# A routing front end moved into the attention before it: batch 0's scores, picks, count and lists made between attention units

## The chip, the cores and the metric

The kernel runs on one NeuronCore of a Trainium2 chip. The metric is the device time in microseconds (us) of one execution. Engines are named as the profile names them: PE is the matrix engine (TensorE; PEld is its load of stationary weights), DVE the vector engine, ACT the scalar engine, POOL the GpSimd engine and SP the engine that issues most DMAs. They run side by side, each its own list of instructions in order, and meet through semaphores.

## The reference

Two batches of 1024 tokens with 256 features go through four layers, each added to its input:

```
x = x + attention0(layernorm(x), ctx)      # 16 heads, 77 context tokens
x = x + slot_mixture(layernorm(x))         # 16 experts, 1024 slots
x = x + attention1(layernorm(x), ctx)      # "second attention": 16 heads, 77 keys
x = x + top3_mixture(layernorm(x))

top3_mixture(x):
  a = x @ P_w.T                            # 64 address features
  dw1, dw2, dw3 = route(a @ U1.T), route(a @ U2.T), route(a @ U3.T)   # 12 experts
  h = gelu(sum_e dw1[:, e] * (x @ W1[e].T))     # 256 -> 1024
  y = sum_e dw2[:, e] * (h @ W2[e].T)           # 1024 -> 256
  return y + dw3 @ b2
route(z): softmax over the 3 largest of 12, zero elsewhere
```

## The kernel before, in words

The tokens are 16 tiles of 128 (8 for each batch), held in `X` for the whole program. The four layers are stages that follow each other. This change is about the end of the third and the beginning of the fourth.

**Second attention** (`attention("a1_", ...)`). A unit is one token tile. There are 16 units; in unit u the tile is u // 2 of batch u % 2, so the batches alternate. Units 4 to 13 stand in a hardware loop, the others are written out. The work of three units overlaps. In step u each engine does, in this order:

- PE (`step`): `scores` of unit u (L827, into `psS`), `input_T` of unit u + 1 (L810), two parts of `probs_T` of unit u - 1 (L843), `output_T` of unit u - 2 (L862), `values` and the last part of `probs_T` of unit u - 1 (L852, L843), `queries` of unit u + 1 (L817), `project` of unit u - 2 (L872).
- DVE (`step`): the four maxima over the scores and their subtraction for unit u (L600, L606), `normalise` of unit u - 1 (L619, L621), `norm_in` of unit u + 2 (L584), `residual` and `stat` of unit u - 2 (L628, L632).
- ACT: copies out of PSUM, the exponential of unit u (L732), then the biased queries of unit u + 1 (L725), which the scores of unit u + 1 need.
- POOL adds the output bias to each tile of `X` (L705) once its normalised input is made.

After unit 15's `probs_T` comes a tail with no next unit to overlap. There DVE also makes the normalisation factors of 14 tiles (`next_begin`, L676), ahead of `normalise` of unit 15. SP loads the weights `W1` of the mixture's first product during this stage.

**The front end of the top-3 mixture** (`route_vector`, `route_tensor`, `route_scalar`, `route_gpsimd`, `route_sync`). A new block of instructions begins when all engines have ended the attention. DVE normalises 16 tiles into `xn` (L1931); PE transposes them (L2005) and multiplies them with the router product `PU` (L2014), two tiles at a time; SP stores `xn` to memory, 1 MB for each batch. For batch 0 DVE then picks the three largest of 12 scores (`pick`, L1604 to L1612), sums the choices (`choose`), PE counts them with triangular and all-ones matrices (`count`, L1622, L1626), DVE works out each token's place in lists sorted by expert (`lists`, L1635 to L1674), compares places with counters (`match_two`, L1713), and PE multiplies these comparisons (`add_tokens`, L1720) so that the list of tokens appears in `psF`. `found_tokens` (L1727 to L1729) turns it into indices and releases POOL, which gathers the rows of `xn` from memory (L1909). Where PE would have nothing to do it runs filler products on weights that nobody reads (`turn_over`, L89).

**The first product** (`expand`, L2133) begins when the first two gathered blocks have been transposed (L2111). It goes through 54 blocks of 128 rows, 8 matmul passes each. What batch 1 needs (picks, count, lists) is made on DVE while batch 0's blocks are multiplied.

## Time and profile before

| | |
|---|---|
| three runs | 1085.78, 1088.67 (median), 1090.91 us |
| profiled execution | 1091.19 us, of which span 1089.3 |
| PE busy | 1038.6 us (95%) |
| DVE busy | 642.7 us (59%) |
| ACT, POOL busy | 401.3 (37%), 282.8 (26%) |
| mean granted PE clock | 0.983 of full |

The span is the time from the first to the last instruction in the trace; the program's own time is 1.9 us longer. A time with a decimal point such as 566.59 is a moment counted from the span's start. The second attention runs from about 447 to 566.6, the front end from 566.6 to 600.3. The granted clock has two levels, 2.4 GHz (1.00 in the rows) and 1.2 GHz (0.50); a value between them is a stretch that held both.

### The profile page before, as it was taken

How to read it: one execution, taken by the hardware profiler on the slowest of the kernel's cores; microseconds unless marked ns; L12 is line 12 of the kernel's file. 1: busy time of each engine (PE TensorE's matmuls, PEld its weight loads, DVE VectorE, ACT ScalarE, POOL GpSimd, SP SyncE). 2: the span in 40 equal slices, each digit the busy share in tenths (PEclk: the TensorE clock that was granted, in tenths of full speed). 3: DMA queues.
4: the chain of work that ended last, by engine and by line, in shares of the span. 5: the costliest groups of instructions: out<-in, count | busy, mean ns of one | idle time of the engine just before them, and what ended most of it. 6: DMA issues, size and time to landing. Idle time of an engine off the chain costs nothing. (4 is left out here: it accounts for less than half of the span.)

```text
span 1089.3 us, 20108 instructions
## 1 busy us (share of the span) xinstructions
PE 1038.6 (95%) x6560; PEld 751.5 (69%) x6560; DVE 642.7 (59%) x1450; ACT 401.3 (37%) x784; POOL 282.8 (26%) x306
## 2 busy tenths in 40 slices
PE   7999989999899999999998999998999999899996
PEld 3788854588899888688875444443347777577784
DVE  3998857777444544567768888665421366534512
ACT  0566644432111222266642355554343222122230
POOL 1211110000021100211111322255533677454431
PEclk8999999999899999999999999999999999999998
DMA  7000040000399200470002444489999999674634
GB/s 232 2 1 0 1 174 18 0 2 1 124 348 343 79 1 0 192 280 0 0 7 90 153 168 174 172 285 358 341 352 405 407 329 346 215 254 146 218 122 169
DMA packets 72057, 177.17 MB, mean 163 GB/s; under 512 B 10605, under 2 KB 31071, under 8 KB 70444
## 3 DMA queue, kind: packets, MB, share of 16 engines
q1 hardware_dynamic: 47362, 102.09, 25.5%
q0 software_dynamic: 20896, 69.75, 18.9%
q10 hardware_dynamic: 3722, 4.33, 1.2%
q8 instruction: 46, 0.75, 0.3%
q14 instruction: 31, 0.25, 0.1%
HBM read 126.06 MB, written 47.97 MB: 160 GB/s over the span
## 5 line engine op out<-in xcount | busy, mean ns | idle before, releaser
L2133 PE MATMUL f_psH<-W,ctxT 128*128 (+2 forms) x216 | 100.6, 610 | 3.9 <-DVE f_stage L2328 2.0
L2232 ACT ACTIVATE shared<-f_psH 128x512 f32<-128x512 f32 x108 | 62.8, 597 | 108.0 <-PE f_psH L2133 75.7
L2182 PE MATMUL f_psT<-W,f_xg 128*128 (+1 forms) x432 | 99.2, 383 | 1.9 <-DVE shared L2477 1.8
L2182 PE MATMUL f_psT<-W,sel 128*64 (+2 forms) x432 | 98.6, 381 | 2.3 <-ACT sel L2257 1.4
L2133 PE MATMUL f_psH<-W,f_xTk 128*128 (+2 forms) x216 | 97.8, 595 | 1.7 <-DVE f_stage L2328 1.0
L2477 DVE COPY shared<-f_psT 128x256 f32<-128x256 f32 x54 | 22.7, 421 | 123.2 <-PE f_psT L2182 97.8
L1909 POOL DMA_INDIRECT f_xg<-xn_d,f_toks x54 | 56.3, 1042 | 130.2 <-PE f_psT L2111 102.4
L2182 PEld LDWEIGHTS f_psT<-W,f_xg 128*128 128x128 f32 (+1 forms) x432 | 79.8, 190 | 13.5 <-issue 3.5
L2182 PEld LDWEIGHTS f_psT<-W,sel 128*64 128x64 f32 (+2 forms) x432 | 62.9, 150 | 27.5 <-issue 5.7
L1909 POOL DMA_INDIRECT f_temps<-h_d,f_toks x54 | 52.8, 979 | 94.6 <-PE f_psH L2161 70.2
L1515 POOL DMA_DIRECT2D m_eos<-m_eo x32 | 16.8, 525 | 201.9 <-DVE m_eo L1412 200.6
L2133 PEld LDWEIGHTS f_psH<-W,ctxT 128*128 128x128 f32 (+2 forms) x216 | 33.9, 167 | 50.5 <-issue 50.5
L2133 PEld LDWEIGHTS f_psH<-W,f_xTk 128*128 128x128 f32 (+2 forms) x216 | 35.8, 175 | 44.7 <-issue 44.6
L705 POOL TENSOR_TENSOR X<-X,a_bob 128x256 f32 x32 | 24.4, 765 | 162.7 <-DVE a_xn L584 82.8
L2068 POOL DMA_INDIRECT p_d<-shared,f_dest x54 | 55.7, 1031 | 34.9 <-DVE shared L2477 20.0
L2257 ACT ACTIVATE sel<-f_psH 128x512 f32<-128x512 f32 x54 | 29.3, 594 | 93.7 <-PE f_psH L2161 93.7
L2257 ACT ACTIVATE f_xg<-f_psH 128x512 f32<-128x512 f32 x54 | 29.3, 595 | 89.8 <-PE f_psH L2161 89.8
L2182 PE MATMUL f_psT<-f_stage,sel 128*32 128x256 f32 (+1 forms) x464 | 62.3, 381 | 0.0
L2410 DVE SCALAR_TENSOR_TENSOR a_W<-f_g,f_wt,a_W 128x1024 f32<-128x1024 f32 x32 | 41.1, 1285 | 34.8 <-DMA f_g<-p_d,f_rows 34.3
L1909 POOL DMA_INDIRECT f_g<-p_d,f_rows x48 | 55.8, 1163 | 20.2 <-issue 13.4
L2161 PE MATMUL f_psH<-ident,f_temps 128*128 128x128 f32 x432 | 57.5, 276 | 2.8 <-DMA f_temps<-h_d,f_toks 1.9
L2161 PEld LDWEIGHTS f_psH<-ident,f_temps 128*128 128x128 f32 x432 | 48.5, 141 | 16.1 <-issue 10.6
(339 smaller groups left out, 2246.6 us busy)
## 6 DMA issues: line engine op xcount, KB each, us to landing
p_d<-shared SPq DMA_DIRECT2D x54, 512.0 KB, 3.3
W<-in_f_W1T SPq DMA_DIRECT2D x12, 1024.0 KB, 17.2
W<-in_f_W2T SPq DMA_DIRECT2D x12, 1024.0 KB, 11.0
m_wg<-in_m_Wg SPq DMA_DIRECT2D x16, 512.0 KB, 4.3
m_wu<-in_m_Wu SPq DMA_DIRECT2D x16, 512.0 KB, 5.7
m_wd<-in_m_Wd SPq DMA_DIRECT2D x16, 512.0 KB, 6.2
h_d<-a_W SPq DMA_DIRECT2D x16, 512.0 KB, 5.9
f_g<-p_d SPq DMA_DIRECT2D x8, 384.0 KB, 7.8
```

The costliest lines, as they stand in the source:

```text
L705: pool.tensor_tensor(X[:, s, j], X[:, s, j], bob[:, :], ALU.add).then_inc(xb_ready, 1)
L1515: pool.dma_start(eos[s * SL:(s + 1) * SL, b, j, :], eo[b * SL:(b + 1) * SL, s, :]).then_inc(eo_moved[s], 16)
L1909: pool.indirect_dma_start(place, None, source, bass.IndirectOffsetOnAxis(ap=index, axis=0)).then_inc(done, 16)
L2068: pool.indirect_dma_start(p2_rows[b], bass.IndirectOffsetOnAxis(ap=dest[:, b * TB + i:b * TB + i + 1], axis=0), y_out[:, n % OUTS, :], Non ...
L2133: mm = pe.matmul(psH[at, n % 2, c, :], xTk[n % 2][:, k, at], weights, start=k == 0, stop=k == KD - 1)
L2161: mm = pe.transpose(psH[:, n % 2, h, k * P:(k + 1) * P], hg[:, n % SEATS, (h * KQ + k) * P:(h * KQ + k + 1) * P], ident[:, :])
L2182: mm = pe.matmul(psT[at, n % 2, 0:D], hT[n % 2][:, k, at], weights, start=k == 0, stop=k == KH - 1)
L2232: act.activation(po[:, n % 2, c * HH:(c + 1) * HH], psH[:, n % 2, c, :], ACT.Copy).then_inc(po_ready, 1)
L2257: act.activation(hT[n % 2][:, h * KQ:(h + 1) * KQ, :].rearrange("p k n -> p (k n)"), psH[:, n % 2, h, :], ACT.Gelu).then_inc(hT_ready, 1)
L2410: sums.step(dve.scalar_tensor_tensor(h, rows_k, wt[:, 0, k, u:u + 1], h, ALU.mult, ALU.add))
L2477: dve.tensor_copy(y_out[:, n % OUTS, :], psT[:, n % 2, 0:D]).then_inc(yo_ready, 1)
```

## The change

The second attention now takes its units batch by batch: unit u is tile u % 8 of batch u // 8, all 16 units written out. An object `Early` is called at fixed places of the unit steps and does batch 0's part of the front end there:

- the router weights are centred (DVE, step 1) and multiplied to `PU` (PE, step 2), so that scores can be made from the raw `X` and scaled afterwards by each token's inverse deviation;
- in steps 3 to 10 PE transposes the finished tile u - 3 of batch 0 along with `output_T`, ACT copies 512 columns where it copied 256, and in steps 4 to 11 PE multiplies a tile with `PU` into free columns of `psO`;
- DVE, after `stat` of the step: factors of batch 0 (step 9), scaling and the first pick (11), second pick (12), third pick and `choose` (13), the starts of the lists (14), shifts and places (15); the count is made by PE in step 14, which waits for `choose`;
- four small constant loads go ahead of `W1` in SP's queue.

In the front end's own block DVE normalises only tiles 0 to 4 and the last two, POOL the other nine; DVE goes at once to `match_two`; PE transposes and scores only batch 1, between its `add_tokens`. All but two fillers go. The first product's second block waits for the copy of batch 1's scores.

The PE's order in an attention step, before (a step of the loop) and then now (the fifth step, unit 4); `a_psP`, `a_psO` and the like are the attention's PSUM and SBUF tiles, and `f_PU` is the router product:

```order
L827 MATMUL a_psS<-shared,a_qT 128x154 x8
L810 MATMUL a_psA<-ident,a_xn 128x128 x2
L843 MATMUL a_psP<-ident,a_pr 128x128 x6
L862 MATMUL a_psP<-ident,a_o 128x128 x2
L852 MATMUL a_psO<-shared,a_pT 128x51 x2
L843 MATMUL a_psP<-ident,a_pr 128x128 x3
L843 MATMUL a_psP<-ident,a_pr 80x128
L852 MATMUL a_psO<-shared,a_pT 128x51 x8
L817 MATMUL a_psA<-a_xnT,a_W 128x128 x4
L872 MATMUL a_psP<-a_W,a_oT 128x256 x2
```
```order
L869 MATMUL a_psS<-shared,a_qT 128x154 x8
L852 MATMUL a_psA<-ident,a_xn 128x128 x2
L885 MATMUL a_psP<-ident,a_pr 128x128 x6
L906 MATMUL a_psP<-ident,a_o 128x128 x2
L911 MATMUL a_psP<-ident,X 128x128 x2
L1913 MATMUL a_psO<-f_PU,a_oT 128x36 x2
L896 MATMUL a_psO<-shared,a_pT 128x51 x2
L885 MATMUL a_psP<-ident,a_pr 128x128 x3
L885 MATMUL a_psP<-ident,a_pr 80x128
L896 MATMUL a_psO<-shared,a_pT 128x51 x8
L859 MATMUL a_psA<-a_xnT,a_W 128x128 x4
L921 MATMUL a_psP<-a_W,a_oT 128x256 x2
```

Two transposes of `X` and two products with `f_PU` have come between `output_T` (L862, now L906) and the first `values` (L852, now L896).

DVE's order at the end of the attention: before from the last step's `residual` on, and now from the last rows of `lists` on (`f_pdiv` and `f_pmod` are what `match_two` compares):

```order
L628 TENSOR_TENSOR X<-a_psP,X 128x256
L632 BN_STATS stats<-X 128x6
L297 MEMSET mhalf 128x2x7
L298 TENSOR_TENSOR mean<-stats 128x2x7
L299 TENSOR_TENSOR mdif<-stats 128x2x7
L300 TENSOR_TENSOR veps<-stats 128x2x7
L302 TENSOR_SCALAR mean<-mean 128x2x7
L303 SCALAR_TENSOR_TENSOR mdif<-mdif 128x2x7
L305 SCALAR_TENSOR_TENSOR vars<-veps,mdif 128x2x7
L308 TENSOR_SCALAR veps<-vars 128x2x7
L619 RECIPROCAL a_rsum<-a_psO 128x16
L621 TENSOR_TENSOR a_o<-a_psO,a_rsum 128x256
```
```order
L1738 CAST f_pdiv<-f_part 128x24
L1739 CAST f_pmod<-f_part 128x24
L301 MEMSET mhalf 128x6
L302 TENSOR_TENSOR mean<-stats 128x6
L303 TENSOR_TENSOR mdif<-stats 128x6
L304 TENSOR_TENSOR veps<-stats 128x6
L306 TENSOR_SCALAR mean<-mean 128x6
L307 SCALAR_TENSOR_TENSOR mdif<-mdif 128x6
L309 SCALAR_TENSOR_TENSOR vars<-veps,mdif 128x6
L312 TENSOR_SCALAR veps<-vars 128x6
L638 RECIPROCAL a_rsum<-a_psO 128x16
L642 TENSOR_TENSOR a_o<-a_psO,a_rsum 128x256
```

Ahead of the block of norm factors (L297 to L308, now L301 to L312) stand now the 23 instructions of `shifts` and `places`, of which the last ones are shown; `normalise` of unit 15 (L619, now L638) stands behind both.

PE's order in the front end, from the end of the count up to the first transposes of gathered rows (L2111, now L2257):

```order
L89 MATMUL f_psT<-W 128x512 x8
L1720 MATMUL f_psF<-f_temps 128x28 x6
L89 MATMUL f_psT<-W 128x512
L1720 MATMUL f_psF<-f_temps 128x28 x6
L89 MATMUL f_psT<-W 128x512
L1720 MATMUL f_psF<-f_temps 128x28 x12
L89 MATMUL f_psT<-W 128x512 x3
L2111 MATMUL f_psT<-ident,f_xg 128x128 x4
```
```order
L89 MATMUL f_psN<-a_W 128x512 x2
L1785 MATMUL f_psF<-f_temps 128x28 x6
L2164 MATMUL f_psT<-ident,f_stage 128x128 x4
L1785 MATMUL f_psF<-f_temps 128x28 x6
L2164 MATMUL f_psT<-ident,f_stage 128x128 x4
L2173 MATMUL f_psH<-f_PU,f_stage 128x36 x4
L1785 MATMUL f_psF<-f_temps 128x28 x6
L2164 MATMUL f_psT<-ident,f_stage 128x128 x4
L2173 MATMUL f_psH<-f_PU,f_stage 128x36 x4
L1785 MATMUL f_psF<-f_temps 128x28 x6
L2164 MATMUL f_psT<-ident,f_stage 128x128 x4
L2173 MATMUL f_psH<-f_PU,f_stage 128x36 x8
L2257 MATMUL f_psT<-ident,f_xg 128x128 x4
```

The fillers on `W` are gone, and batch 1's transposes (L2164) and scores (L2173) stand between the `add_tokens` (L1720, now L1785) of batch 0.

The diff, cut to its core:

```diff
+                def at(j, s):
+
+                    return (s, j) if first else divmod(B * j + s, NT)
...
+                                early.evict(dve, u, room)
...
+                                early.vector(dve, u, stat_done)
...
+                            add_biases(0, NT + 4)
+                            early.power(pool)
+                            add_biases(NT + 4, TT)
...
+                            if routed(u - 1):
+                                pe.wait_ge(y_done, u)
+                                for k in range(KD):
+                                    mm = pe.transpose(psP[:, 0, (KD + k) * P:(KD + k + 1) * P],
+                                                      X[:, 0, u - 1, k * P:(k + 1) * P], ident[:, :])
...
+                    PLACES = 6
+                    CENTRE, PRODUCT, FACTORS, PICKS, COUNT = 1, 1, 9, 11, 13
...
+                    def tensor(self, pe, u, room, oT, oT_ready):
+                        if u == self.PRODUCT:
+                            pe.wait_ge(pw_step, 3)
+                            for k in range(KD):
+                                mm = pe.matmul(room[:, k * R * E1:(k + 1) * R * E1], Pw[:, k * P:(k + 1) * P], U[:, :],
+                                               start=True, stop=True)
+                            mm.then_inc(pu_mm, 1)
+                        i = u - 3
+                        if 0 <= i < NT:
+                            pe.wait_ge(oT_ready, u - 1)
+                            pe.wait_ge(pu_ready, 1)
+                            for k in range(KD):
+                                mm = pe.matmul(room[:, self.column(i)], oT[:, u % B, KD + k, :], PU[:, k, :],
+                                               start=k == 0, stop=k == KD - 1)
+                            mm.then_inc(z0_mm, 1)
+                        if u == self.COUNT:
+                            pe.wait_ge(consts, 2)
+                            count(pe, room, chosen_ready, 1).then_inc(count_mm, 1)
...
+                    def evict(self, dve, u, room):
+                        if u == self.PRODUCT:
+                            dve.wait_ge(pu_mm, 1)
+                            dve.tensor_copy(PU[:, :, :].rearrange("p k n -> p (k n)"), room[:, 0:KD * R * E1]
+                                            ).then_inc(pu_ready, 1)
+                        if u == self.PLACES + 2:
+                            self.copy_scores(dve, room, 0, self.PLACES)
+                        if u == NT + 2:
+                            self.copy_scores(dve, room, self.PLACES, NT)
+                        if u == self.COUNT:
+                            dve.wait_ge(count_mm, 1)
+                            steps_of.step(dve.tensor_copy(counts[:, :], room[:, 0:(NT + 1) * E1]), hold=False)
...
+                        if u == self.CENTRE + 2:
+                            dve.wait_ge(ld, 16 * 4)
+                            one.step(dve.tensor_tensor(
+                                under[:, :, :], iota[:, 0:E1 + 1].unsqueeze(2).to_broadcast([P, E1 + 1, E1]),
+                                iota[:, 0:E1].unsqueeze(1).to_broadcast([P, E1 + 1, E1]), ALU.is_gt))
+                        if u == self.FACTORS:
+                            dve.wait_ge(stat_done, NT)
+                            begin0(dve)
+                        if u == self.PICKS:
+                            end0(dve)
+                            dve.wait_ge(z0_ready, 2)
+                            one.step(dve.tensor_tensor(
+                                Z[:, :, 0:NT, :], Z[:, :, 0:NT, :],
+                                rstd[:, 0:NT].unsqueeze(1).unsqueeze(3).to_broadcast([P, R, NT, E1]), ALU.mult))
+                        if self.PICKS <= u < self.PICKS + TOP:
+                            pick(dve, one, 0, 0, 0, NT, range(u - self.PICKS, u - self.PICKS + 1))
+                        if u == self.PICKS + TOP - 1:
+                            choose(dve, one, 0, 0)
+                            dve.sem_inc(chosen_ready, 1)
+                        if u == self.COUNT + 1:
+                            one.hold()
+                            starts(dve, one, counts)
+                        if u == self.COUNT + 2:
+                            shifts(dve, one, counts)
+                            places(dve, one, 0, 0)
+
+                second_attention(Early())
...
+                    BY_VECTOR = 5
+                    SHARES = ((BY_VECTOR, NT - BY_VECTOR), (BY_VECTOR + 2, TT - 2 - BY_VECTOR))
...
                     def route_vector(dve, one):
 
-                        def norm_in(u):
-                            dve.tensor_scalar(xn[:, u, :], Xf[:, u, :], mean[:, u:u + 1], rstd[:, u:u + 1],
-                                              ALU.subtract, ALU.mult).then_inc(xn_ready, 1)
-
-                        for u in range(2):
-                            norm_in(u)
+                        for u in range(BY_VECTOR):
+                            norm_in(dve, u, xn_ready)
                         begin(dve)
-                        for u in range(2, NT - 1):
-                            norm_in(u)
-                        end(dve)
-                        for u in range(NT - 1, TT):
-                            norm_in(u)
-                        dve.wait_ge(ld, 16 * 4)
-                        one.step(dve.tensor_tensor(
-                            under[:, :, :], iota[:, 0:E1 + 1].unsqueeze(2).to_broadcast([P, E1 + 1, E1]),
-                            iota[:, 0:E1].unsqueeze(1).to_broadcast([P, E1 + 1, E1]), ALU.is_gt))
-                        dve.wait_ge(z_mm, NT // 2)
-                        one.step(dve.tensor_copy(Z[:, :, 0:NT, :].rearrange("p r t e -> p t r e"),
-                                                 psZ[:, 0, 0:HZ].rearrange("p (t r e) -> p t r e", r=R, e=E1)))
-                        pick(dve, one, 0, 0, 0, NT)
-                        choose(dve, one, 0, 0)
-                        dve.sem_inc(chosen_ready, 1)
-                        dve.wait_ge(count_mm, 1)
-                        lists(dve, one, psN, 0, 0)
                         for i in range(0, NT, 2):
                             match_two(dve, i, at_hit, iota, pdiv, at_used).then_inc(hit_ready, 2)
                             match_two(dve, i, at_row, iota, pmod, at_used).then_inc(row_ready, 2)
...
                         for i in range(NT):
                             act.wait_ge(hit_ready, i + 1)
                             wait(act, at_used, i - AR + 1)
                             act.activation(at_tile[:, i % AR, :, 0, :], at_hit[:, i % AR], ACT.Copy, scale=tokid[:, i:i + 1]
                                            ).then_inc(tile_ready, 1)
+                            if i % 2:
+                                inputs_T(i // 2)
+                        act.wait_ge(z_mm, NT // 2)
+                        act.activation(Z[:, :, NT:TT, :].rearrange("p r t e -> p t r e"),
+                                       psZ[:, 0, 0:HZ].rearrange("p (t r e) -> p t r e", r=R, e=E1), ACT.Copy
+                                       ).then_inc(z_copied, 1)
...
+                        for u in range(BY_VECTOR, NT):
+                            norm_in(pool, u, xn_by_pool)
                         power(pool)
-                        pool.memset(ones_b[:, :], 1.0).then_inc(consts, 1)
-                        pool.wait_ge(ld, 16 * 4)
-                        pool.tensor_copy(below_b[:, :], below).then_inc(consts, 1)
+                        for u in range(NT, TT - 2):
+                            norm_in(pool, u, xn_by_pool)
...
+                        turn_over(pe, psN[:, :], W_flat, 2)
                         pe.wait_ge(w1_ld, 16 * E1)
-                        pe.wait_ge(consts, 2)
-                        count(pe, psN, chosen_ready, 1).then_inc(count_mm, 1)
-                        turn_over(pe, psT[:, 0, :], W, 8)
                         for i in range(NT):
                             pe.wait_ge(row_ready, i + 1)
                             pe.wait_ge(tile_ready, i + 1)
                             add_tokens(pe, i, 1, psF, at_used)
-                            if i % 2 and i < NT - 3:
-                                turn_over(pe, psT[:, 0, :], W, 1)
+                            if i % 2:
+                                inputs_T(i // 2)
+                                if i > 1:
+                                    scores(i // 2 - 1)
+                        scores(NT // 2 - 1)
 
```

## Rows read from the trace of the kernel before

**Rows 1.** Windows: stretch, length, busy PE PEld DVE ACT POOL, PE clock, DMA share, GB/s
```profile
483.49:551.53 68.04, 66.92 (x621) 58.75 (x620) 48.42 (x99) 41.10 (x90) 6.86 (x10) 1.00 0.00 0
551.53:566.59 15.06, 13.64 (x100) 10.76 (x99) 8.70 (x25) 5.48 (x12) 2.60 (x1) 1.00 0.00 1
566.59:600.30 33.71, 28.66 (x167) 18.38 (x168) 28.02 (x104) 8.53 (x20) 6.05 (x8) 0.93 0.26 81
```
**Rows 2.** Timeline, one loop unit: start, length, engine, line, operation, idle before
```profile
483.73 0.42 DVE L628 TENSOR_TENSOR X<-a_psP,X 128x256 f32 x1 [0.81 <-PE a_psP L872]
...
484.65 1.62 DVE L600 TENSOR_REDUCE a_mx<-a_psS 128x4 f32<-128x308 f32 x4
...
485.69 0.55 PE L852 MATMUL a_psO<-shared,a_pT 128*128 128x51 f32 x4
...
486.30 1.44 DVE L606 TENSOR_TENSOR a_sc<-a_psS,a_mx 128x1232 f32<-128x1232 f32 x1
...
487.94 1.23 ACT L732 ACTIVATE a_pr<-a_sc 128x1232 f32<-128x1232 f32 x1 [0.56 <-DVEq L612]
...
488.56 0.26 DVE L619 RECIPROCAL a_rsum<-a_psO 128x16 f32<-128x16 f32 x1 [0.81 <-PE a_psO L852]
...
489.20 0.41 DVE L584 TENSOR_SCALAR a_xn<-X,mean,rstd 128x256 f32 x1
...
489.60 0.63 ACT L725 ACTIVATE a_qT<-a_psA,a_bq 128x128 f32<-128x128 f32 x2 [0.43 <-PE a_psA L817]
...
490.28 0.81 PE L827 MATMUL a_psS<-shared,a_qT 32*128 32x154 f32 x16
```
**Rows 3.** Timeline, a unit outside the loop
```profile
476.68 0.81 PE L827 MATMUL a_psS<-shared,a_qT 32*128 32x154 f32 x16
...
477.58 1.62 DVE L600 TENSOR_REDUCE a_mx<-a_psS 128x4 f32<-128x308 f32 x4
```
**Rows 4.** Timeline: first gather, first two blocks of the first product
```profile
594.96 1.16 POOL L1909 DMA_INDIRECT f_xg<-xn_d,f_toks  x1 [23.27 <-DVEq L1959]
...
600.30 4.88 PE L2133 MATMUL f_psH<-W,ctxT 128*128 x8 [0.29 <-issue]
...
605.24 3.60 PE L2133 MATMUL f_psH<-W,f_xTk 128*128 x8
```
**Rows 5.** Timeline, weight loads of two successive score groups, front end
```profile
571.45 0.97 PEld L2014 LDWEIGHTS f_psH<-f_temps,f_stage 128*128 128x128 f32 x8
...
572.73 0.97 PEld L2014 LDWEIGHTS f_psH<-f_temps,f_stage 128*128 128x128 f32 x8
```
**Rows 6.** Timeline, DVE: factors, picks, choices, list starts, shifts
```profile
567.26 0.15 DVE L298 TENSOR_TENSOR mean<-stats 128x2 f32<-128x2 f32 x1
...
575.71 0.25 DVE L1604 TENSOR_REDUCE f_wt<-f_temps 128x8 f32<-128x96 f32 x1
...
581.87 0.17 DVE L1635 TENSOR_SCALAR f_cnt<-f_psN 128x12 f32<-128x12 f32 x1 [0.67 <-PE f_psN L1626]
...
584.21 0.15 DVE L1645 TENSOR_SCALAR f_base<-f_start 128x1 f32<-128x1 f32 x1
...
587.18 0.46 DVE L1667 TENSOR_TENSOR f_temps<-f_temps,sel 128x288 f32<-128x288 f32 x1
```
**Rows 7.** Timeline, DVE: unit 15 is normalised, attention's tail
```profile
561.74 0.26 DVE L619 RECIPROCAL a_rsum<-a_psO 128x16 f32<-128x16 f32 x1 [2.42 <-PE a_psO L852]
```
**Rows 8.** Timeline, DVE: two successive pairs of comparisons
```profile
589.04 0.33 DVE L1713 TENSOR_TENSOR f_temps<-f_iota,f_pdiv 128x168 f16<-128x168 f32 x1
...
590.16 0.33 DVE L1713 TENSOR_TENSOR f_temps<-f_iota,f_pdiv 128x168 f16<-128x168 f32 x1
```
**Rows 9.** Timeline, POOL: a bias added, two factors raised to a power
```profile
476.18 0.73 POOL L705 TENSOR_TENSOR X<-X,a_bob 128x256 f32 x1 [6.12 <-DVE a_xn L584]
...
568.30 0.92 POOL L315 TENSOR_TENSOR rstd<-veps,mhalf 128x2 f32<-128x2 f32 x1 [6.30 <-DVE veps L308]
```
**Rows 10.** Timeline, ACT: two comparisons are scaled
```profile
589.47 0.62 ACT L1985 ACTIVATE f_temps<-f_temps,f_tokid 128x84 f16<-128x84 f16 x2 [9.12 <-DVE f_temps L1713]
```

207 lines of the change are left out of this document (137 added, 70 removed).

## The prediction

> **What bounds the kernel now.** I read the windows first, to see which engine fills each stretch, and then single units of the timeline, to see what releases what. In the ten loop units of the second attention (483.49 to 551.53) [rows 1] PE is busy 66.92 of 68.04 us, DVE 48.42. A unit costs 6.8 us, and at first sight DVE has 2 us free in each. The unit itself says otherwise [rows 2]: the reader is to follow one chain through three engines. The reduction starts at 484.65, the exponential 3.29 us later, it lasts 1.23, ACT's two query copies can start then, and the next scores follow 0.68 behind their start (489.60 to 490.28). So the next scores come at the earliest 3.29 + 1.23 + 0.68 = 5.2 us behind the reduction. The copies started 0.43 us behind the exponential's end, released by PE: the chain is that close to binding. Outside the loop [rows 3] the reduction starts 0.90 us behind its own scores, so chain (6.1) against PE (6.8) leaves 0.7 us. The written-out form is what the new kernel has.
>
> The front end, from 566.59 [rows 1], lasts 33.71 us and is a line on DVE: 28.02 us busy. Its end is the first gather at 594.96, 28.4 us in, and the first block of the product 5.3 us later [rows 4].
>
> **PE in the attention.** Eight times two transposes and two products with `PU` are added. Two score groups of two tiles, with the transposes between them, stand 1.28 us apart (571.45 to 572.73) [rows 5], so a tile costs 0.64 us: 8 x 0.64 = 5.1 us. They stand in PE's own list, which has no room to hide them. The product `PU` itself I take as 0.3 us (bounds 0 and 0.5: four passes like those of rows 5). The copies that ACT makes longer stay beside PE's work. The four constant loads go ahead of `W1` on SP, and nothing before the front end waits for `W1`: nothing.
>
> **DVE in the attention.** All pieces stand between `stat` and the next reduction. Free are 0.7 us of them; what goes beyond delays the next scores one for one. A second delay in a row is smaller, since PE ends `project` while it waits and the next `residual` is then early.
>
> - Step 9, factors: 567.26 to POOL's release at 568.30, 1.04 us [rows 6, 9]. PE's unit is 0.64 longer there, so it hides.
> - Step 11: scaling 0.46 (row 587.18, the same 288 elements) and a pick. Three picks and `choose` are 19 instructions from 575.71 to 581.20 (581.87 less the 0.67 of waiting for PE), 0.29 each [rows 6]. A pick of six is 1.74. Together about 2.25 us: the reduction is 3.15 behind its scores, the unit lasts 3.15 + 5.2 = 8.35: +1.55.
> - Step 12: six more, 1.74. DVE has ended `norm_in` 4.2 us behind its reduction (3.09 to the subtraction's end, 1.05 for `normalise` and `norm_in`) [rows 2], at 7.35; with 0.92 for `residual` and `stat` and the 1.74 the reduction stands at 10.0 - 8.35 = 1.65: the unit is 6.85: nothing.
> - Step 13: seven instructions, 2.0 us. The reduction of step 14 is 2.9 us late in its unit. PE comes to the count 2.2 us in, as it comes to `values` now (485.69, scores 0.24 ahead of 483.73 [rows 1, 2]), waits 0.8 and counts; DVE waited 0.67 for a count with both signals [rows 6], of which I take 0.5 (bounds 0 and 0.67): the unit is 8.15: +1.35.
> - Step 14: list starts, 581.87 to 584.21, 2.34 us [rows 6]. The last reduction is 3.3 us behind its scores in place of 0.9.
> - Step 15: shifts and places, 584.21 to 589.04, 4.83 us [rows 6, 8], and then the 1.04 of factors, all ahead of `normalise` of unit 15. Counted from the last scores: subtraction's end 6.4, `normalise` 7.1, `residual` and `stat` 8.05, shifts and places 12.9, factors 13.95. Now this `normalise` starts at 561.74 [rows 7], 10.2 behind the scores at 551.53. Here ends last not PE but DVE: +3.7.
>
> DVE's sum is 1.55 + 1.35 + 3.7, rounded 6.7 with the copies that `evict` adds, and the attention grows by 5.1 + 0.3 + 6.7 = 12.1 us.
>
> **The front end.** Counted from its start, five normalisations are 1.7 us (two now take 566.59 to 567.26 [rows 1, 6]), factors to 2.7. Pairs of comparisons follow 1.12 apart [rows 8], the last done at 7.2. But PE's list is in order and mixes batch 1 in. `inputs_T` of its first tiles waits for POOL's fifth normalisation. The trace has no such operation on POOL; its two-input add of the same shape takes 0.73 [rows 9], the nearest row, which I take. Bounds: DVE's 0.41 for the same work [rows 2], and twice 0.73. Three by 2.3, the power of 0.92 us behind the factors at 3.7, the fifth at 5.2. Then transposes to 5.8 (0.3 to 0.5 us, the 1.28 of rows 5 less the products), ACT's copy to 6.5 (taken as long as two scalings, 0.62 [rows 10]), its two scalings to 7.1, two `add_tokens`, the second transposes and first scores to 8.8, ACT's next two scalings to 9.2, again adds, transposes, scores to 10.9, last scalings 11.3, last adds 11.6; the indices and the gather at 12.75. Before it was 28.4: -15.6 us. With POOL at 0.41 it is 0.6 us better, at 1.46 3.9 worse (the ninth normalisation then comes at 14.1). The store of `xn` can start by 2.5 and has ten microseconds. Gather to product stays 5.3: batch 1's last scores end at about 13.9, before the gathered rows land.
>
> On POOL the Trainium skill, "GPSIMD Engine Reference", "Engine selection", says that two-input elementwise work runs at about half VectorE's speed and one-input work at roughly line rate. The trace agrees on the first (0.73 against DVE's 0.42 for an add) and no run here shows the second; by that rule the lower bound would hold, and the sum be 0.6 us better.
>
> **The sum.** +12.1 - 15.6 = -3.5 us. Behind the first block nothing changes: PE fills what follows, and the DVE work for batch 1 hangs on the same list. Against the profiled execution, 1091.19 us (span 1089.3 and 1.9 around it), that is 1087.7; the median of the three runs is 2.5 us lower, so the forecast is 1085.2 us. A measurement of this kernel can't tell less than 0.5%, 5.4 us, from no change.
>
> **The rivals.**
>
> *The DVE pieces hide.* For it: 20 us idle in the ten units. If PE absorbs steps 11 to 14 (the reduction may be late where PE has other work), the attention pays PE's 5.4, the count's 0.5, and in the tail shifts, places and factors from 6.5 to 12.4 against 10.2, 2.2 us: 8.1. Then 8.1 - 15.6 = -7.5, 1081.2 us: faster. Against it: the 0.43 us of rows 2.
>
> *The clock falls.* The front end has a mean granted clock of 0.93 [rows 1], so part of it ran at 1.2 GHz, and the first block behind it, after a stretch with little PE work, took 4.88 us where the next took 3.60 [rows 4]. The fillers that stood there are gone, and the attention's end gets new holes of 2.4 and 3.7 us. If the clock is low from the attention's tail to the second block: about 6 us of PE's serial work in the tail at half speed, half of it on the path, +3; fillers, adds, two transposes and two score groups on the way to the list, 4.4 us, doubled, +4.4; one more slow block, 3.6 in place of the 1.28 lost now, +2.3. From -3.5 to +6.2: 1094.9, slower. It decides from a fall before the front end; a fall only behind the list costs at most the 2.3. Against it: the tail now has 1.4 us of PE idle [rows 1] at clock 1.00.
>
> The Trainium skill, "TensorE: Matmul & The Clock Gate", "HAM oscillation — how this bites in real kernels", has gaps in TensorE's work throttle it again, and each return is paid anew. The trace agrees that the clock falls in the stretch with the thin work [rows 1, 4]; by the rule this rival's price is due.
>
> *The list was not what the front end waited for.* If the store of `xn`, or POOL's other work, or a slow POOL holds the gather, most of the gain is lost: with POOL at 1.46 us the sum is +0.4, 1089.1. For it: nine normalisations are moved to an engine that reads the same memory as DVE; against: DVE's own list was 28 us long and its end released the gather.
>
> **How the numbers follow.** Forecast 0.55, its own range 1081.5 to 1089.5; hidden pieces 0.22; clock 0.12; POOL or store 0.11. Faster by over 0.5%: the hidden case and 0.07 of the forecast's edge, 0.29. Slower: the clock case and 0.01, 0.13. Within: 0.58. The range reaches to the hidden case's far side and the clock case: 1078.5 to 1094.
>
> **What would show it.** The attention, from the scores of unit 4 to the block change, 12 us longer, with units of 7.4 us in steps 4 to 10, two of over 8 us in steps 12 and 14, and `normalise` of unit 15 behind DVE's factors instead of released by PE. The first gather 12 to 13 us into the front end, PE's adds waiting for ACT's scalings, POOL's normalisations 0.7 us each. Wrong would be: units that stay at 6.8; a last `normalise` released by PE; a clock of 0.50 before the front end.

## The result, and the profile after

The changed kernel is slower: 1097.75 us (median of five runs, 1090.70 to 1100.31) against 1088.67; the ratio is 1.0062, 95% interval [1.0032, 1.0091]. The forecast was 1085.2 with a range to 1094.0. Repeated twice with twelve runs each, the same kernel gave 1.0039 [1.0016, 1.0061] and 1.0047 [1.0027, 1.0067]. So it is slower by 0.4 to 0.6%, where a gain of 0.3% was forecast. One execution of the first kernel with fillers (1200.87 us, mean granted clock 0.841) and one of the first kernel with split normalisations (1114.59 us, 0.969) are left out of the ratios below.

The kernel before was run again beside each kernel, and its median moved from 1088.67 up to 1105.10 us between these sets, so ratios are compared below, and times only within one set.

The profiled execution took 1090.70 us, span 1088.5, which is less than before's 1089.3. The other four runs took 1096.2 to 1100.3, with mean granted clocks of 0.970 to 0.973 where the profiled one had 0.981. This profile shows one part of the loss; the other needs a profile of a longer execution, which came with the repetition.

First the attention. These rows are PE's of the changed kernel: scores of units 10, 11, 13, 14 and 15, and the first instruction of the front end.

```profile
521.13 0.81 PE L869 MATMUL a_psS<-shared,a_qT 32*128 32x154 f32 x16
528.64 0.81 PE L869 MATMUL a_psS<-shared,a_qT 32*128 32x154 f32 x16
...
544.17 0.81 PE L869 MATMUL a_psS<-shared,a_qT 32*128 32x154 f32 x16 [1.31 <-ACT a_qT L763]
551.07 0.81 PE L869 MATMUL a_psS<-shared,a_qT 32*128 32x154 f32 x16
559.23 0.81 PE L869 MATMUL a_psS<-shared,a_qT 32*128 32x154 f32 x16
...
577.66 1.95 PE L89 MATMUL f_psN<-a_W 128*128 128x512 f32 x4 [0.30 <-PEq L569]
```

A middle unit lasts 7.51 us (528.64 less 521.13; 6.8 before [rows 1]), step 12 lasts 8.22 (544.17 less 535.95; forecast 8.35), step 13 lasts 6.90 (551.07 less 544.17; forecast 6.85), step 14 lasts 8.16 (forecast 8.15), and the tail from the last scores to the front end 18.43 (15.06 before). From the first scores (449.21; 450.80 before) to the front end it is 128.45 us against 115.79: +12.7, where the sum had +12.1.

Then the windows of the changed kernel (columns: stretch, length, then busy time and, in brackets, number of instructions of PE, PEld, DVE, ACT and POOL, granted clock, DMA share, GB/s) and PE's timeline in the front end.

```profile
577.66:583.50 5.84, 2.30 (x10) 0.93 (x10) 5.71 (x19) 0.62 (x2) 5.81 (x5) 1.00 0.18 60
583.50:600.73 17.23, 12.39 (x70) 11.08 (x71) 8.11 (x26) 4.95 (x13) 12.39 (x12) 0.51 0.40 129
600.73:604.50 3.77, 3.77 (x5) 1.70 (x6) 3.32 (x14) 0.13 (x1) 1.85 (x2) 0.51 0.36 107
```

```profile
582.05 0.35 PE L1785 MATMUL f_psF<-f_temps 128*128 128x28 f16 x6 [2.44 <-DVE f_temps L1778]
586.36 1.11 PE L2164 MATMUL f_psT<-ident,f_stage 128*128 128x128 f32 x4 [3.96 <-POOL f_stage L2102]
588.50 0.49 PE L1785 MATMUL f_psF<-f_temps 128*128 128x28 f16 x6 [1.03 <-ACT f_temps L2134]
588.84 1.10 PE L2164 MATMUL f_psT<-ident,f_stage 128*128 128x128 f32 x4
589.72 1.76 PE L2173 MATMUL f_psH<-f_PU,f_stage 128*128 128x36 f32 x8
...
600.73 5.52 PE L2281 MATMUL f_psH<-W,ctxT 128*128 x8 [0.30 <-issue]
```

PE stood 3.96 us before its first transposes, released by POOL's normalisation, and from 583.5 on it ran at 1.2 GHz (0.51): the scores of two tiles took 1.76 us in place of 0.98 (the row below is of before), the first block 5.52 in place of 4.88 [rows 4].

```profile
571.55 0.98 PE L2014 MATMUL f_psH<-f_temps,f_stage 128*128 128x36 f32 x8
```

The first gather started 17.8 us into the front end and the first block 23.1, in place of 12.75 and 18.1. So the front end gave 10.6 us (33.71 less 23.07), not 15.6.

POOL's normalisations answer to the 0.73 of [rows 9]. One line for all nine (durations in ns, minimum, median, maximum), and the two slowest from the timeline:

```profile
L2102 POOL TENSOR_SCALAR f_stage<-X,mean,rstd x9: 1213/1222/2566, 577.7 to 589.9; 128x256 f32<-128x256 f32 x9
```

```profile
582.54 2.57 POOL L2102 TENSOR_SCALAR f_stage<-X,mean,rstd 128x256 f32<-128x256 f32 x1
...
589.90 1.66 POOL L2102 TENSOR_SCALAR f_stage<-X,mean,rstd 128x256 f32<-128x256 f32 x1
```

The one of 2.57 us ran while DVE made comparisons (from 580.76 to 584.2), the one of 1.66 beside DVE's last pair. Those for which DVE stood still took 1.21 to 1.22.

Between the two profiled executions +12.7 (attention), -10.6 (front end) and +0.6 (first block) make +2.6 us. The rest of the 0.8 by which the changed span is the shorter one lies in code that is the same in both: 1.6 ahead of the first scores, 1.9 behind the second block.

### The profile page after: what moved, and what is told of

The parts are those of the page before. It is cut to its first block and busy times, and to the rows that moved or that the text cites. A ratio compares the mean times of both kernels' runs of the same rounds, so it can differ in the third digit from the quotient of the medians.

```text
span 1088.5 us, 19787 instructions
## 1 busy us (share of the span) xinstructions
PE 1030.2 (95%) x6534; PEld 750.4 (69%) x6534; DVE 641.4 (59%) x1456; ACT 399.1 (37%) x779; POOL 295.7 (27%) x316
## 5 line engine op out<-in xcount | busy, mean ns | idle before, releaser
L2625 DVE COPY shared<-f_psT 128x256 f32<-128x256 f32 x54 | 22.7, 422 | 124.6 <-PE f_psT L2330 99.2
L2215 POOL DMA_INDIRECT p_d<-shared,f_dest x54 | 55.6, 1030 | 34.2 <-DVE shared L2625 19.4
L2085 POOL DMA_INDIRECT f_g<-p_d,f_rows x48 | 54.6, 1137 | 17.6 <-issue 12.8
L1414 PE MATMUL m_psE<-m_eos,m_wu 128*128 128x256 f32 x256 | 57.8, 380 | 0.4 <-DVE m_wu L1490 0.4
```

What stands on the lines that cost most here:

```text
L1414: mm = pe.matmul(psY[:, s, 0:D], ecT[:, s, c, :], eos[:, s, c, :], start=c == 0, stop=c == CS - 1)
L2085: pool.indirect_dma_start(place, None, source, bass.IndirectOffsetOnAxis(ap=index, axis=0)).then_inc(done, 16)
L2215: pool.indirect_dma_start(p2_rows[b], bass.IndirectOffsetOnAxis(ap=dest[:, b * TB + i:b * TB + i + 1], axis=0), y_out[:, n % OUTS, :], Non ...
L2625: dve.tensor_copy(y_out[:, n % OUTS, :], psT[:, n % 2, 0:D]).then_inc(yo_ready, 1)
```

## The experiments

Two theories. **A, the clock:** the attention's tail and the front end hold too little work for PE, the granted clock falls to half, and the longer executions have more of it. **B, POOL:** its slow normalisations hold PE and the list. Each ratio is to the kernel before, with its 95% interval, of twelve runs where nothing else is said. Times "in" count from the start of the front end.

**The changed kernel again, twice.** No edit.

> The changed kernel once more, unaltered. Its four runs without a profile were at 1096.2 to 1100.3 us with a mean granted clock of 0.970 to 0.973, the profiled one at 1090.7 us with 0.981. Theory A (the clock: the front end falls to half clock, and most runs hold a further stretch of it that the profiled one did not have): the median stays at 1096 to 1100 us, mean clocks again fall into two groups, and a profile from the slow group shows a stretch of 15 to 25 us at 0.50 that the first profile does not have. Theory B (GpSimd's slow normalisations alone cost the time): one group of clocks and the same median. Here the two are only told apart if the profile comes from the slow group.

> The changed kernel unaltered, for its groups of runs beside those of the next two on one chip. Theory A: two groups again, 6 us apart, the slower with mean clocks 0.005 lower; if the profile falls into it, it shows the half clock for 13 us from PE's 1.92 us wait on, and 22.5 us from the last scores to the front end in place of 18.4. Rival: a slow profile with a short fall in the tail, and the missing clock elsewhere.

The first gave nine runs from 1091.5 to 1094.2 (mean clocks 0.975 to 0.978) and three from 1098.3 to 1098.9 (0.972 to 0.974); its profile came from the faster ones and looks like the first (18.44 us from the last scores to the front end). The second gave six runs of 1090.5 to 1095.6 and six of 1096.6 to 1099.1 (0.970 to 0.974), and its profile, 1097.07 us, fell among the latter. In the mean the groups are 6.1 and 4.2 us apart (expected: 6). Its windows around the tail, and PE in it:

```profile
559.00:568.90 9.90, 7.77 (x67) 6.46 (x67) 8.16 (x23) 4.93 (x9) 0.00 (x0) 1.00 0.01 2
568.90:582.40 13.50, 12.93 (x45) 9.98 (x46) 7.70 (x38) 2.40 (x6) 1.33 (x1) 0.52 0.00 0
```

```profile
561.11 0.81 PE L869 MATMUL a_psS<-shared,a_qT 32*128 32x154 f32 x16
...
568.77 0.95 PE L885 MATMUL a_psP<-ident,a_pr 128*128 128x128 f32 x6 [1.92 <-ACT a_pr L770]
...
571.83 3.49 PE L896 MATMUL a_psO<-shared,a_pT 128*128 128x51 f32 x16
575.12 2.04 PE L921 MATMUL a_psP<-a_W,a_oT 128*128 128x256 f32 x4
...
579.95 3.45 PE L89 MATMUL a_psS<-a_W 128*128 128x512 f32 x4
583.69 1.96 PE L89 MATMUL f_psN<-a_W 128*128 128x512 f32 x4 [0.30 <-PEq L569]
```

PE waits 1.92 us for the last exponents, and then its clock is 1.2 GHz for 13 us: products that take 2.00 us at full speed take 3.49, and the front end starts 22.58 us behind the last scores in place of 18.43: 4.15 us. In the first profile the same wait was followed by the same fall, but for 3 us only:

```profile
567.50:570.50 3.00, 3.00 (x18) 2.89 (x16) 2.72 (x15) 1.27 (x4) 0.00 (x0) 0.53 0.00 0
570.50:577.66 7.16, 5.97 (x30) 3.89 (x29) 4.32 (x21) 1.02 (x3) 1.33 (x1) 1.00 0.00 0
```

There it cost nothing, since DVE's shifts and places ended last anyway: with the clock at 1.00 throughout the tail is as long, 18.43 us (below). Of the ten profiles taken with this wait left open, five had the short fall and five the long one. The long fall explains the mean clocks too: 10.5 us more at half clock are 0.005 of the span. What makes it long or short in one execution I did not find. The front ends of the two profiles are alike (first gather 17.8 us in both). Their spans differ by 6.4 us: 4.15 in the tail, 1.9 ahead of the first scores (451.07 against 449.21), in code that no kernel here changes and where the profiles range from 448.6 to 451.9, and the small rest behind the tail.

**POOL's normalisations on DVE.**

```
-  BY_VECTOR = 5
+  BY_VECTOR = NT              # all of batch 0 on DVE
   for i in range(0, NT, 2):   # ahead of each pair of comparisons
+      if i < NT - 2:
+          for u in range(NT + i, NT + i + 2):
+              norm_in(dve, u, xn_ready)
-  for u in range(BY_VECTOR, NT):
-      norm_in(pool, u, xn_by_pool)
-  for u in range(NT, TT - 2):
-      norm_in(pool, u, xn_by_pool)
```

> All 16 normalisations of the front end on VectorE (8 of the first batch, then 2 of the second batch ahead of each pair of comparisons), none on GpSimd. Theory B: PE's first transposes no longer wait for GpSimd (3.96 us in the changed kernel's profile), the list is ready when VectorE's chain allows (8 x 0.42 + 1.1 + 3 x 2.0 + 1.2 = 11.7 us, so first gather about 14 us into the front end in place of 17.8), and the median falls by 3 to 4 us. Theory A: the clock stays at 0.50 from about 6 us into the front end, the pairs on PE still take 3.2 us each, the gather comes 16 to 17 us in, and the median falls by 1 us or less.

1.0000 [0.9978, 1.0022], median 1089.61 where the changed kernel beside it had 1092.76. PE's wait for POOL is gone and the gather is at 14.05 us in (591.51 less 577.46):

```profile
583.07 0.64 PE L2160 MATMUL f_psT<-ident,f_stage 128*128 128x128 f32 x4
584.74 0.49 PE L1785 MATMUL f_psF<-f_temps 128*128 128x28 f16 x6 [1.03 <-ACT f_temps L2137]
585.07 1.09 PE L2160 MATMUL f_psT<-ident,f_stage 128*128 128x128 f32 x4
...
591.51 1.16 POOL L2085 DMA_INDIRECT f_xg<-xn_d,f_toks  x1 [9.37 <-DVEq L2121]
```

The transposes show the clock fall between 583 and 585. B's 3 to 4 us are there (3.7 in the gather, 3.15 in the medians), and with them the change costs nothing; A alone would have given 1 or less.

**Fillers in the front end.** Passes over weights that nobody reads, with POOL's normalisations kept, and then with them on DVE.

```
-  turn_over(pe, psN, W_flat, 2)
+  turn_over(pe, psN, W_flat, 4)      # with DVE's normalisations: 7
   ...
+  turn_over(pe, psN, W_flat, 4)      # behind the second addition (POOL's form only)
   scores(NT // 2 - 1)
+  turn_over(pe, psN, W_flat, 1)
```

> Idle stretches of PE in the front end filled with multiplications of weights that nobody reads: 2 more passes (1 us each) before the first addition of tokens, 4 after the second, 1 at the end; GpSimd keeps its normalisations. Theory A: the granted clock stays at 1.00 through the front end, a pair on PE takes 1.9 us in place of 3.2, the first gather comes 3 to 4 us earlier (14 to 15 us in), the first block takes 4.9 us in place of 5.5, and the median falls by 4 to 8 us, the runs' mean clocks rising above 0.98. Theory B: the gather still waits for GpSimd's last normalisation (it ends 13.8 us in), so it comes at 15 us at the earliest, the clock alone saves 1 to 2 us.

> Both edits: all normalisations on VectorE, and 5 more filling passes on PE before the first addition (PE would wait about 5 us there), 1 at the end. If both theories hold their parts add: the gather comes 13 to 14 us in, the first block starts 20 us into the front end (23.1 in the changed kernel) and takes 4.9 us, and the median falls by 4 to 6 us, to 1092 to 1094. If only the clock counts, it equals the kernel with fillers alone; if only GpSimd counts, the kernel with VectorE's normalisations alone.

1.0051 [1.0023, 1.0080] and 1.0002 [0.9972, 1.0032]: no gain over the same kernels without fillers, where A had 4 to 8 us. But neither kernel is the test that it was meant to be, since the clock did not stay up until the gather. It stood at 1.00 for the first 9 us or more and then fell. With POOL's normalisations (first two rows) it fell about where PE waited 1.24 us for POOL, and with DVE's (last two) between 590 and 592; the scores of two tiles, 0.98 us at full clock, then took 1.76:

```profile
596.12 1.12 PE L2164 MATMUL f_psT<-ident,f_stage 128*128 128x128 f32 x4 [1.24 <-POOL f_stage L2102]
597.02 1.76 PE L2173 MATMUL f_psH<-f_PU,f_stage 128*128 128x36 f32 x8
```

```profile
592.17 1.08 PE L2160 MATMUL f_psT<-ident,f_stage 128*128 128x128 f32 x4
593.05 1.76 PE L2169 MATMUL f_psH<-f_PU,f_stage 128*128 128x36 f32 x8
```

The gather came at 18.35 us in with POOL's normalisations and at 14.07 with DVE's (17.8 and 14.05 without fillers). So a full clock ahead of the third pair of tiles is worth nothing, as PE then waits for POOL between the pairs (0.24, 1.24) or for DVE. What the half clock costs behind it comes from a later kernel: from the third transposes to the gather it is 3.82 us in the changed kernel (591.61 to 595.43) and 3.13 in the last form below, at full clock. With POOL on the path the clock is thus worth about 0.7 us there, an estimate from these two profiles; no run kept POOL's normalisations and held the clock. The filler behind the last scores stood in the way of the gathered tokens: gather to first block took 6.05 us in both, in place of 5.3 and 5.4. Both profiles also had the 13 us fall in the tail (22.7 and 22.6 us).

**The tail.** First PE's 1.92 us wait filled, alone and with DVE's normalisations; then also the wait for the last normalised output, which was then 1.68 us long.

```
+  turn_over(pe, psA, Wq, 2)
   probs_T(NT - 1, B - 1, U - 1, 0)
   ...
+  turn_over(pe, psA, Wq, 2)          # second form only
   output_T(NT - 1, B - 1, U - 1, 4 * U)
```

> One edit to the changed kernel: PE's wait of 1.92 us for the last unit's exponents, in the attention's tail, is filled with two passes over weights that nobody reads. Theory A (that wait drops the clock: for 3 to 4 us in two profiles, for 13 us in the profiles of the two kernels with fillers in the front end, whose attention is the same): the clock stays at 1.00 to the end of the attention, the front end starts 0.5 to 1.5 us earlier than in the profiles with the short fall (577.0 in place of 577.7 to 579.0), the slower group of runs (3 of 12 at 1098.3 to 1098.9, the rest 1091.5 to 1094.2) thins out, and the median falls by 1 to 2 us. Rival (the half clock follows from the idle time in the units ahead, or from the clock's own rhythm): it falls all the same, no change in start or median.

> All normalisations on VectorE and the tail's wait filled. The two effects add if both are real: VectorE's normalisations alone gave 1089.6 (median) against 1092.8 of the changed kernel; with the tail's clock held it should be 1087.5 to 1088.5, and its upper group of runs (1092.7 to 1094.7, 3 of 12) gone. If the filler does nothing: 1089.6 again.

> The changed kernel with both of PE's waits in the attention's tail filled, two passes each over weights that nobody reads: the one for the last exponents (1.92 us) and the one for the last normalised output (1.68 us once the first is filled, and where the clock then fell for 4 us). Theory A: the clock stays at 1.00 up to the front end, the time from the last scores to the front end is 18.4 to 18.7 us (18.4 with the short fall of the changed kernel's profile, 19.8 with the first wait filled alone, 22.7 where the fall was 13 us long), the runs lose their slower group (upper end below 1096, mean clocks above 0.976), and the median is 1 to 4 us below the changed kernel's in proportion to before (ratio about 1.003 or less). Rival (the slow group is made elsewhere): the same two groups as before, ratio 1.004 to 1.006.

One wait filled: 1.0058 [1.0027, 1.0088] (seven runs) and 1.0020 [0.9999, 1.0041], no gain in either, against the forecasts of 1 to 2 us each. The clock stayed up through the filled wait and fell in the next one, where a fall is on the path: 19.80 and 19.79 us from the last scores to the front end. Both filled: 18.43 us, at full clock throughout:

```profile
560.00:577.94 17.94, 16.67 (x102) 11.64 (x95) 14.20 (x55) 5.53 (x12) 1.33 (x1) 1.00 0.00 1
```

and 1.0030 [1.0005, 1.0055]. Thirteen of the changed kernel's 29 runs had a mean clock below 0.975; with both waits filled, three of twelve. The intervals overlap, so the gain in time is not shown by this ratio alone. And the low clocks are not all gone, as was expected: two of the twelve were at 1115 us and 0.971, so the tail is not the only place where time at half clock comes and goes.

**Shifts and places to the front end,** in the changed kernel and with the first wait filled.

```
-  if u == self.COUNT + 2: shifts(...); places(...)   # attention, step 15
   begin(dve)
+  shifts(dve, one, counts)                           # front end
+  places(dve, one, 0, 0)
```

> One edit to the changed kernel: the first batch's shifts and places (22 VectorE instructions, 4.9 us) leave the attention's last step and stand in the front end, ahead of the comparisons. If they cost the attention what the sum said (3.7 us in the tail), the front end starts at 573.5 to 574.5; there the first comparison comes 4.9 us later on VectorE, but PE waits for GpSimd's normalisations until 8.7 us in and to 13.8 us in anyway, so the gather moves little (18 to 20 us in) and the median falls by 1.5 to 3.5 us. If they were hidden in the attention (rival), the start stays at 577.7 and the median rises by 1 to 5 us. If the clock follows PE's wait in the tail, the low stretch there goes too, since the last exponents no longer... stand behind that work: no effect either way, as the work is issued after them.

> The changed kernel with shifts and places in the front end and PE's 1.92 us wait filled. From the last scores to the front end: 15.06 us before, 18.43 in the changed kernel. If shifts and places carry the whole difference, as the prediction's sum had it, 14.8 to 15.1 us. If the starts in the step ahead carry part (they put the last reduction off, and with it the exponents, for which PE waits until 7.67 us after the scores in place of 5.60), PE's own chain gives 7.67 + about 9 = 16.6 us. The whole kernel is no faster than the changed one, since the comparisons start 4.9 us later on VectorE: first gather 18 to 20 us into the front end, ratio 1.003 to 1.007.

The first, 1.0065 [1.0041, 1.0088], was profiled with the long fall, in which PE sets the tail: 22.75 us, which says nothing of shifts and places. Its gather came 19.15 us in, as expected, but the fall of the median by 1.5 to 3.5 us did not come. The second (1.0031 [1.0008, 1.0054], ten runs) kept its clock in the tail. Three rows of PE: last scores, first work on the last exponents, front end:

```profile
558.60 0.81 PE L869 MATMUL a_psS<-shared,a_qT 32*128 32x154 f32 x16
...
566.27 0.88 PE L885 MATMUL a_psP<-ident,a_pr 128*128 128x128 f32 x6 [0.20 <-ACT a_pr L770]
...
575.24 1.95 PE L89 MATMUL f_psN<-a_W 128*128 128x512 f32 x4 [0.30 <-PEq L569]
```

16.64 us. So of the tail's 3.37 us, 1.6 are left without shifts and places, and 1.8 come from these. The 1.6 come from the steps ahead: the last exponents are ready 2.1 us later behind their scores than before, and in the changed kernel's trace DVE makes the list starts just ahead of the last reduction (559.98 to 562.3). No run took the list starts alone away.

**The order of units alone.** The kernel before, with one batch behind the other and nothing else of the change.

```
-  dve.tensor_tensor(X[:, s, j], psP[:, 1, 0:D], X[:, s, j], ALU.add)
+  b, i = divmod(B * j + s, NT)       # and so in norm_in, stat, scores, values
+  dve.tensor_tensor(X[:, b, i], psP[:, 1, 0:D], X[:, b, i], ALU.add)
```

> The kernel before with one part of the change: the second attention takes one batch behind the other, and everything else (the routing, its place, the front end) stays as it was. The prediction put this part at nothing: attention 115.8 us from the first scores to the front end, median within 1.5 us of before. Rival: the order itself costs (GpSimd's additions of the bias, the factors of the last tiles, a unit's buffers), then the attention is more than 1 us longer. Since the routing's pieces are missing from the attention, PE's waits in it are those of before, and theory A wants the clock at 1.00 through its tail.

1.0004 [0.9984, 1.0025]. Attention 116.3 us (449.01 to 565.28) against 115.8, since every unit now lasts 6.85, where a loop unit took 6.80. The tail is 15.05 us, at clock 1.00:

```profile
550.23 0.81 PE L851 MATMUL a_psS<-shared,a_qT 32*128 32x154 f32 x16
565.28 1.10 PE L89 MATMUL f_psN<-sel 77*128 77x512 f32 x2 [0.30 <-PEq L562]
```

**Half of the routing product.**

```
-  for k in range(KD):  # transposes of X, and products with PU
+  for k in range(1):
```

> Leaves out half of the routing scores' product in the attention: one transpose and one multiplication of 128 rows in place of two each, so the first batch is routed otherwise and only the attention's part of the trace is read. The sum took the product at 0.64 us a unit, on PE's path (8 units, 5.1 us). If so, the units of steps 5 to 10 shrink from 7.51 to 7.1 to 7.25 us. Rival (another engine sets the units' length): 7.51 again.

```profile
485.84 0.81 PE L869 MATMUL a_psS<-shared,a_qT 32*128 32x154 f32 x16
493.03 0.81 PE L869 MATMUL a_psS<-shared,a_qT 32*128 32x154 f32 x16
```

7.19 us a unit in place of 7.51: half of the product is 0.32, as the sum had it.

**One operation in place of two on POOL.**

```
-  tensor_scalar(xn, X, mean, rstd, subtract, mult)
+  tensor_scalar(xn, X, mean, None, subtract)       # POOL's nine tiles only
```

> The changed kernel with GpSimd's normalisations cut to the subtraction of the mean (the multiplication by the factor is left out in those nine tiles). If each operation of the two costs GpSimd a pass: 0.7 to 0.8 us each in place of 1.22. If the instruction's form costs the same whatever it computes: 1.2 us again.

```profile
L2103 POOL TENSOR_SCALAR f_stage<-X,mean x9: 921/949/1774, 579.7 to 589.4; 128x256 f32<-128x256 f32 x9
```

This is one run, read from its trace. 0.95 us, between the two expectations: the second operation costs 0.27, the first with its per-partition operand already more than an add of two tiles (0.73). PE's wait for POOL ahead of its first transposes falls from 3.96 to 1.87 us and the gather from 17.8 to 15.75 us in (595.40 less 579.65): the gather follows the price of this one instruction.

**POOL only where nobody waits.** It keeps three normalisations of batch 0, which only the store needs; DVE takes five, and all of batch 1. Then the same with both tail waits filled (run twice), and last with PE's waits in the front end filled too (3 passes ahead of the first addition, 1 ahead of the third).

> GpSimd keeps only the three normalisations of the first batch, in which nothing waits for it; VectorE takes 5 of the first batch and all of the second. With all on VectorE the first gather came 14.05 us into the front end, VectorE's chain of 3.4 + 1.1 + 3 x 2.0 + 1.2 us and the rest ahead of it; three fewer take 1.25 us off: gather 12.8 us in, product 18.2 us in, ratio to before 0.9985 to 0.9995 (0.5 to 1.5 us better than all on VectorE, which was level with before). Rival (GpSimd's work slows VectorE's, or the store of the first batch is late): gather at 14 us or later, ratio 1.000 or above.

> Both edits. If the tail's clock and GpSimd's normalisations are the two causes, this is the best form of the change: attention's end held at full clock, gather 12.8 us in, median 1 to 3 us below before (ratio 0.997 to 0.999), upper group gone. If the tail's clock does not matter: equal to the split alone.

> The split of the normalisations with the attention's tail held at full clock, once more for its ratio: 0.997 to 0.999 of before, one group of runs. If the first ratio (0.998, interval 0.9958 to 1.0003) was luck: 1.000 to 1.002.

> The same with PE's waits in the front end filled too: 3 passes of 1 us ahead of the first addition (PE waited 3.23 us), one ahead of the third (1.03 us). If the half clock costs the front end time: clock 1.00 to the gather, which comes 11.9 to 12.8 us in (13.84 before), the first block starts 17.3 to 18.3 us in (19.4) and takes 4.9 us (6.2); median 1.5 to 3 us under the kernel without them, ratio 0.995 to 0.997. Rival (VectorE's chain and the transfers set the gather anyway, or the clock falls elsewhere instead): gather at 13.8, equal medians.

0.9985 [0.9962, 1.0007]; with the tail held 0.9980 [0.9958, 1.0003] and 0.9995 [0.9976, 1.0014]; with the front end filled 0.9977 [0.9961, 0.9992], median 1087.89 against 1090.62. The last form is the only one whose interval lies below 1, by little, and its ratio is short of the 0.995 to 0.997 that was expected. The gather missed its forecast of 12.8 us in as long as the front end was not filled: 13.85, 13.84 and 13.84. DVE, which makes the indices, waits 2.52 us there for PE's last additions, at half clock; with the front end filled it waits 1.23. With the split alone, five of eleven runs had a mean clock below 0.975; with the tail held too, one of twelve in the same set. That points to the tail as the place of the low clocks, though the two ratios cannot be told apart. The last form's profile is of its longest execution, 1093.77 us, so only the stretches shown are read from it; whether its first block is as long in a median execution is not known. Its windows and rows:

```profile
561.00:577.32 16.32, 15.18 (x84) 10.54 (x82) 12.71 (x48) 4.68 (x11) 1.33 (x1) 1.00 0.00 1
577.32:590.90 13.58, 12.24 (x84) 8.34 (x84) 11.91 (x36) 4.52 (x12) 5.82 (x6) 1.00 0.41 136
590.90:600.00 9.10, 6.02 (x12) 2.58 (x12) 8.09 (x32) 1.73 (x4) 4.93 (x6) 0.51 0.42 124
```

```profile
589.88 1.18 POOL L2089 DMA_INDIRECT f_xg<-xn_d,f_toks  x1 [7.73 <-DVEq L2125]
...
595.64 6.49 PE L2285 MATMUL f_psH<-W,ctxT 128*128 x8 [0.30 <-issue]
```

The gather is at 12.56 us in (13.84 without the fillers, at half clock) and the first block at 18.3 (19.4). The fall has moved behind the gather, where PE waits 2.25 us for the rows, and the first block pays for it: 6.49 us.

## Why the prediction was wrong

*What held.* The attention's terms. The product costs 0.64 us a tile (half of it 0.32). Steps 12, 13 and 14 were forecast at 8.35, 6.85 and 8.15 and are 8.22, 6.90 and 8.16. The whole attention was forecast at +12.1 and is +12.7. The order of units, put at nothing, costs 0.5 us of that (units of 6.85 for loop units of 6.80), which no ratio shows (1.0004). In the tail the +3.7 is 3.4, and DVE ends last there, as forecast (PE's last `output_T` waits 0.38 us for `normalise`); shifts and places carry 1.8 of it, what stands ahead of them 1.6.

*The step that failed first: POOL at 0.73 us a normalisation, "Three by 2.3 ... the fifth at 5.2".* A normalisation takes POOL 1.22 us, up to 2.57 beside DVE's comparisons. The fifth ended 8.7 us in (586.36 less 577.66), forecast at 5.2, and the gather was at 17.8 in place of 12.75. With POOL off the path it is 13.84 to 14.05, so 3.7 to 3.9 us of the 5.0 are this term, and with POOL's instruction cut to 0.95 us it is 15.75. The upper bound of 1.46, with its price of 3.9, was about right: it had the ninth normalisation at 14.1, and it ended 13.9 in. The rule of the Trainium skill in "GPSIMD Engine Reference", "Engine selection", one-input work at roughly line rate, does not hold here: 1.22 us against DVE's 0.41. My error was to take the nearest row, an operation of another form, and to leave out what DVE does to POOL meanwhile.

*The second: the clock, left out of the forecast.* The remaining 1.3 us of the gather (13.84 against 12.56) is the half clock in the front end; with POOL on the path it costs the gather about 0.7, by the estimate above. The 0.6 in the first block may be the same, but it is the difference of two profiles, and in those with the same front end the block took 4.88 to 6.09 us. In the profiles with the long fall the tail adds 4.15. The rival had the mechanism, a fall from the attention's tail on, with +3, +4.4 and +2.3. Its +3 was 4.15 in such runs and 0 in the others, its +4.4 was 1.3 with POOL off the path and about 0.7 behind POOL, its +2.3 was 0.6. What spoke against it, 1.4 us of idle PE at clock 1.00 in the tail of before, was weak: the longest single wait in it was 0.52 us, and the change puts one of 1.92 there. That this wait matters is shown: the clock fell behind it in all ten profiles that left it open, and ran through it at 1.00 in all seven that filled it. The rule of "HAM oscillation — how this bites in real kernels" in "TensorE: Matmul & The Clock Gate" of the Trainium skill, that gaps in TensorE's work throttle it again, agrees with these ten profiles.

*The sum as measured:* +12.7 - 10.6 + 0.6 = +2.6 us, and 0 to 4.15 for the tail's long fall: +2.6 to +6.8. The three ratios are +4.2 to +6.8 us. Why the fall lasts 3 us in one execution and 13 in another stays open. Four of the first five runs had the low mean clocks, against nine of the 24 that followed. By the two repetitions (1.0039 and 1.0047 of 1088.67) the time would have been 1092.9 and 1093.8, just inside the range: that it fell outside is partly the luck of five runs; that the sign was wrong is not. The range itself stopped at 1094 although the clock rival it was to cover stood at 1094.9.

The forecast of -3.5 was also thin for its chances: its case and the hidden pieces, the two of the four with a gain, had 0.77 together. It was the difference of two sums of 12 and 16 us, one of which stood on an operation that the trace did not hold. The rivals' terms could also come together, as they did: the slow POOL and the clock were priced each alone.

## What to carry to other kernels

When work moves from the critical engine to another, price it by a row of the same form on that engine, and else by the upper bound, since the engines that wait in order behind it pay the difference. A wait that a change opens for the matrix engine is not over when it ends: look at the granted clock behind it in several profiles, of longer executions too, and fill every wait of a short serial tail or none: here a fall that was kept from the wait of 1.92 us came in the next, of 1.68, and the tail was 19.8 us in place of 18.4. When a profile is faster than its kernel's median, profile again until one is like the median. And before a filler is called useless, look whether the clock stayed up to the end of the stretch that it was to help.

## What was not expected of the hardware

- POOL took 1.22 us for a normalisation of 128x256 (DVE 0.41), 0.95 for the subtraction alone, 0.73 for an add of two tiles; and 2.57 for one beside DVE's comparisons.
- After the same 1.92 us wait the clock was 1.2 GHz for 3 us in some executions and for 13 in others, and products went from 2.00 to 3.49 us.
- One wait filled (1.88 us of passes) only moved the fall some 7 us on, to the next wait of 1.68 us; with both filled the tail's 18.4 us ran at 1.00 in all four profiles taken.
